# Packing the first two value parts of heads 1 to 7 into dense bf16 rows on the scalar engine, in a two-layer graph kernel

## What is computed

```
feats   = x @ W[h]                                     # 8 heads of 64 units
dense   = leaky_relu(e_self[i] + e_neigh[j], 0.2)      # e_* = feats . a_*
att     = softmax(dense where adj is 1)                # over j
x       = layernorm(x + relu(att @ feats + b))         # layer 0, heads side by side
agg     = adj @ x / max(rowsum(adj), eps)
x       = layernorm(x + relu(concat(x, agg) @ W1.T))   # layer 1
```

## Time and profile before

| what | us |
|---|---|
| median of three runs | 3327.2 |
| the profiled execution, its own time | 3327.12 |
| its span, first to last instruction | 3325.3 |
| PE busy (matmuls) | 3233.3 |
| PE weight loads busy | 2747.0 |
| vector engine busy | 2353.1 |
| scalar engine busy | 1866.8 |
| GpSimd busy | 283.5 |
| mean granted TensorE clock | 0.996 |

### The profile page before, as it was taken

One profiled execution on the slowest core, in us unless ns is written; L12 is line 12 of the kernel. 1 busy time (PEld: TensorE's weight loads), 2 busy tenths in 40 slices (PEclk: granted clock), 3 DMA queues, 4 the chain that ended last, 5 costly groups with the idle time before them and its releaser, 6 DMA issues.

```text
span 3325.3 us, 124497 instructions
## 1 busy us (share of the span) xinstructions
PE 3233.3 (97%) x56896; PEld 2747.0 (83%) x56896; DVE 2353.1 (71%) x4236; ACT 1866.8 (56%) x2456; POOL 283.5 (9%) x251
## 2 busy tenths in 40 slices
PE   4999999999999999999999999999999999999998
PEld 3978879788796978969789697897978879697895
DVE  3857858587685867858678585785858758587685
ACT  2746647365564655646466474664746647465563
POOL 0020100202002020010200102010020200202001
PEclk8999999999999999999999999999999999999999
DMA  6235251341514315252162422525135151441501
GB/s 180 73 64 149 62 138 55 92 128 57 143 61 105 108 50 151 67 111 89 50 157 67 113 88 59 150 64 131 64 79 140 57 143 50 105 119 51 135 32 51
DMA packets 368653, 314.48 MB, mean 95 GB/s; under 512 B 285056, under 2 KB 285056, under 8 KB 368128
## 3 DMA queue, kind: packets, MB, share of 16 engines
q1 hardware_dynamic: 368128, 306.52, 34.1%
HBM read 205.26 MB, written 34.08 MB: 72 GB/s over the span
## 4 chain that ended last, share of the span: by engine, by line
PE 84%; DVE 7%; DMA 5%; ACT 2%; issue 1%; SPq 0%; DVEq 0%; POOL 0%; ACTq 0%
PE six L889 73%; PE pair L889 10%; DVE mask L727 2%; DMA s_bc<-self_scores 2%; DMA out_dram<-mask 1%; DMA self_scores<-sc_row 1%; PE pair L918 1%; DVE rest L635 1%; PE six L918 1%; DVE x_parts L631 1%; ACT trh L462 1%; DVE feat L669 1%; ACT step L497 1%; DMA adj_t<-adj_word 0%; DVE trl L664 0%
## 5 line engine op out<-in xcount | busy, mean ns | idle before, releaser
L889 PE MATMUL six<-x_parts,mask 128*128 128x65 bf16 x16384 | 1547.9, 192 | 21.1 <-DVE mask L727 21.1
L889 PEld LDWEIGHTS six<-x_parts,mask 128*128 128x128 fp8e4 x16384 | 1536.8, 97 | 30.2 <-issue 20.5
L889 PE MATMUL six<-third,mask 128*128 128x65 bf16 x16384 | 1547.7, 192 | 1.9 <-issue 1.6
L889 PE MATMUL six<-rest,mask 128*128 128x65 bf16 x16384 | 1548.0, 195 | 1.3 <-issue 1.2
L889 PEld LDWEIGHTS six<-third,mask 128*128 128x128 fp8e4 x16384 | 1537.0, 98 | 2.5 <-issue 2.4
L889 PEld LDWEIGHTS six<-rest,mask 128*128 128x128 fp8e4 x16384 | 1531.7, 96 | 1.7 <-issue 0.8
L497 ACT ACTIVATE step<-s_bc,n_step 128x1024 uint16<-128x1024 f32 x1024 | 1089.1, 1137 | 378.3 <-DVE mask L727 344.7
L727 DVE TENSOR_TENSOR mask<-adj_t,step 128x1024 uint16<-128x1024 uint16 x1024 | 649.9, 685 | 60.5 <-ACT step L497 60.5
L889 PE MATMUL six<-adj_t,x_parts 128*128 128x512 fp8e4 x1536 | 385.2, 379 | 16.2 <-DVE trl L857 5.4
L440 POOL TENSOR_TENSOR s_bc<-feat,rden 128x512 f32<-128x512 f32 x112 | 124.6, 1118 | 2789.9 <-DVE s_bc L770 2776.2
L889 PEld LDWEIGHTS six<-adj_t,x_parts 128*128 128x128 f16 x1536 | 144.8, 98 | 206.1 <-issue 19.6
(11 more groups left out here) (125 smaller groups left out, 4566.9 us busy)
## 6 DMA issues: line engine op xcount, KB each, us to landing
s_bc<-self_scores SPq DMA_DIRECT2D x128, 512.0 KB, 3.8
mask<-in_adj_dram SPq DMA_DIRECT2D x64, 512.0 KB, 4.5
xs<-in_x_dram SPq DMA_DIRECT2D x128, 256.0 KB, 4.2
adj_nat<-in_adj_dram SPq DMA_DIRECT2D x64, 512.0 KB, 4.3
out_dram<-mask SPq DMA_DIRECT2D x128, 256.0 KB, 3.5
adj_nat<-in_x_dram SPq DMA_DIRECT2D x64, 256.0 KB, 5.8
step<-in_x_dram SPq DMA_DIRECT2D x64, 256.0 KB, 3.9
xs<-in_L_gnn_W_dram SPq DMA_DIRECT2D x1, 2048.0 KB, 12.3
```

The costliest lines, as they stand in the source:

```text
L889: return pe.matmul(o, l, r, start=start, stop=stop, skip_group_check=True)
```

## The change

From head 1 on (`PACKED_FROM = 1`) the scalar engine copies the first and the second part of each value into dense bf16 rows with a step of 66 numbers (132 bytes) from row to row. The tensor engine reads these in place of the upper halves. Head 0 still reads the upper halves, and the third part is as before. Each copy waits for the vector pass that makes its source (`val_f32`, `val_rest`). The two copies of head h stand on the scalar engine ahead of the step that comes five behind the mask after which the vector engine makes these values: ahead of steps 11, 17, 25, 33, 41, 49 and 57. The tensor engine waits for both before the head (`val_packed`). The first part has a buffer of its own, `packed`, and the second lies in `adj_word`, which is idle during the heads. `wa32` moves into `key_w`, which frees 256 bytes. `VALUES_AT` lists the places of the value parts, and these do not move.

```diff
@@ constants
+    PACKED_FROM = 1
...
+    VALUES_AT = {(h - 1) * T + (4 if h > 1 else 6): h for h in range(1, H)}
...
+        ROW_BF = U1 + 1
+        packed = [rows_of.rearrange("p (s k t u) -> p s k t u", s=2, k=2, t=T)[:, :, :, :, 0:U1] for rows_of in (
+            sb("packed", [P, 4 * T * ROW_BF], BF16)[:, :],
+            adj_word[:, :, :].rearrange("p s n -> p (s n)")[:, 0:4 * T * ROW_BF].bitcast(BF16))]
...
-        wa32 = sb("wa32", [P, KC, SC], F32)
+        wa32 = key_w[:, 0].rearrange("p t h -> p (t h)").rearrange("p (c n) -> p c n", c=KC)
...
+        val_packed = signal("val_packed", 2 * (H - PACKED_FROM))
@@ scalar engine
+                def pack_values(h):
+                    for part, made in enumerate((val_f32, val_rest)):
+                        act.wait_ge(made.sem, made.at(b, h + 2))
+                        copy(packed[part][:, h % 2], val[h % 2][part]).then_inc(val_packed.sem, 1)
...
                 for g in range(H * T):
+                    if g - STEP_SLOTS - 1 in VALUES_AT and VALUES_AT[g - STEP_SLOTS - 1] >= PACKED_FROM:
+                        pack_values(VALUES_AT[g - STEP_SLOTS - 1])
                     make_step(g)
@@ vector engine
-                    if jt == (4 if h else 6) and h < H - 1:
-                        value_parts(b, h + 1)
+                    if g in VALUES_AT:
+                        value_parts(b, VALUES_AT[g])
@@ tensor engine
+                    parts = val[h % 2]
+                    if h >= PACKED_FROM:
+                        parts = (packed[0][:, h % 2], packed[1][:, h % 2], parts[2])
...
-                                         val[h % 2][part][:, kind, jt, :],
+                                         parts[part][:, kind, jt, :],
...
                     pe.wait_ge(val_p2.sem, val_p2.at(b, h + 2 if h else 1))
+                    if h >= PACKED_FROM:
+                        pe.wait_ge(val_packed.sem, val_packed.at(b, 2 * (h - PACKED_FROM + 1)))
```

## The result

The changed kernel takes 3294.4 us (median of four runs, 3292.6 to 3296.2) against 3327.0 (four runs): a ratio of 0.9909, 95% interval 0.9896 to 0.9921. That is 32.5 us faster, less than half of the 67 us forecast, though inside the stated range and of the forecast sign. It lies 6 us above the rival "only the byte rate counts" (3288), and so between this rival and the free stride (3327), not between it and the forecast.

What follows compares the result with a forecast made beforehand. PE was taken as the bound, by the pitch of its 65-column matmuls in the heads. From 3327.1 us, 69 less for dense operands and 1.5 more for late masks, copies free, gave 3260 us; 8-in-10 range 3235 to 3333.

Steps and rivals of the forecast that it cites:

- only the byte rate counts: Rival for the strided matmuls of heads 1 to 7: gain only 40 us, time 3288 us; chance 0.16.
- the free stride: Rival: the 4-byte step costs nothing, something all three matmuls share sets the pitch, time 3327 us; chance 0.19.
- That PE's pitch is the time of the heads, and the moving operand's step part of it: Heads: 2064 matmuls without break, 31.21 ns each, 27.1 ns of columns; part of the rest is the operands' 4-byte step.
- The rival of a pitch that the weight load alone sets: Free-stride rival: pitch set by something shared, foremost the 98 ns weight load of each matmul; 3327 us, chance 0.19.
- The size of the stride's price: Triples of heads 1 to 7: 93.6 to 88.8 ns, 4.8 ns less, times 14336, 69 us gained.
- The 227 against 216 ns of the earlier trace: Hint from 512-column matmuls: fp32r products 227 ns against dense 216; as a rate, 1.4 ns a strided 65-column matmul.
- What is late next: Head 3, mask 29: its 0.45 us lead shrinks by 0.38 over five tiles; charged 0.1 us a batch, 1.5 in all.
- The scalar copies: Scalar engine, 224 copies of 1.15 us each, lying in idle time during the vector engine's value passes, costing nothing.
- The rival of slow copies: Rival: copies take 2.3 us each, the scalar engine becomes the bound, 3364 us; slower case in all 0.12.
- the worse reading of rows at 132 bytes: PE might read rows 132 bytes apart worse than the third part's at 144; folded into the slower case, 0.12.
- The wait of PE for masks: PE waits for a mask only at the head of a batch, 21.1 us in the run, and stays near that.
- my third hint: Inside a tile, gaps of 0.04, 0.04 behind the second part against 0.02, 0.03 behind the dense third; called weak.

## Why the prediction was wrong

**That PE's pitch is the time of the heads, and the moving operand's step part of it: right.** The rule of the Trainium skill, SBUF — State Buffer, section Door 1: The DMA port swizzle, by which a 4-byte step is free because four accesses fall in one 16-byte line, does not hold for PE's moving operand here: 1.5 ns for each 65 columns, on average over the key tiles. The rival of a pitch that the weight load alone sets falls with the same runs, since the loads stayed and the pitch fell; a share of the load in the dense 30.2 ns is not excluded.

**The size of the stride's price: the step that failed first.** I took a dense 65-column matmul at 27.1 + 2.5 = 29.6 ns, the 2.5 from 512-column streams, and gave all that was above it, 2.4 ns a matmul, to the two strided operands. Measured are 30.2 ns for a dense one and 1.5 for the step. The term was 69 us and is 44. The 227 against 216 ns of the earlier trace rows gave a nearer price (1.4 ns). I set it aside since its weights were fp32 as well, and gave the 40 us only 0.16. As no run shows that those 11 ns are the price of the stride, that it came so near may be luck. The error was to take a remainder for a price: what was above a floor carried over from matmuls eight times as long went to the one suspect I had.

**"What is late next": the second step that failed.** I charged 1.5 us, from the lead of mask 29 in the second batch and five tiles of head 3. The vector engine's chain was thought to start anew from PE's sums at each head. In heads 1 to 3 it does not: with the extra x_low passes and their 1.37 us waits it goes at a pace of its own. From mask 21, the first behind value parts, to mask 29 it is 534.54 - 521.69 = 12.85 us, and in the kernel before the same, 336.97 - 324.04 = 12.93 in the second batch and 12.85 in the third; from mask 13 to mask 21 it is 12.85 too. From tile 13 to tile 21, with two transposes on the way, PE took 8 x 1.5 + 2 x 0.47 = 12.9 us, and takes 8 x 1.45 + 0.94 = 12.5 now. From tile 21 to tile 29, with none, it took 12.0, and now has work for 11.6. In the fourth batch masks 13, 21 and 29 were there 1.06, 1.18 and 0.32 us before PE began their tiles. Now the first two are there 0.78 and 0.48 us before, and PE stands 0.83 us longer than a usual distance ahead of tile 29. Since both engines start afresh at tile 7, where PE waits for the mask, PE gains over the 21 tiles from 8 to 29, not over five: 21 x 16 x 3.1 ns = 1.04 us. At the 4.8 ns of the forecast it would have been 1.6 us a batch against a lead of 0.3, so at its own pitch the prediction should have charged some 1.3 us a batch, not 0.1. Of 7.8 us it foresaw 1.5. Two experiments bear on the cause: with the copies made and not read there is no standing at tile 29, and with the trh copies one step earlier, and nothing else changed, it is gone. It takes both the faster PE and the vector engine's wait for trh.

**The scalar copies: right in size (1.08 us against 1.15), place and cost (nothing).** The rival of slow copies falls with that; so does the worse reading of rows at 132 bytes.

**PE standing inside tiles: not in the prediction at all.** It cost 4.7 us more than before. The wait of PE for masks, which the prediction kept near 21 us, is 23.4 us in the view of waits; part of the standing at tile 29 goes there by another name.

## What to carry to other kernels

Price a change of an operand's form by the difference of two streams that differ in this form, and not by what is left above a floor; where only the remainder is at hand, test on paper what it gives when half of it belongs to something else. When the bound gets faster, follow each engine that feeds it over the whole stretch until it next waits for the bound; a lead that is there in one tile may be what is left of one that shrinks over three heads. A price per operand that is an average over places should be carried over as an average alone.

## What the runs showed that was not expected

**PE stands inside tiles, the longer in all the faster it goes.** The matmul starts of the changed kernel around one such place, in the second batch (start us, us, what):

```profile
314.56 0.20 PE L906 MATMUL six<-adj_word,mask 128*128 128x65 bf16 x1
314.60 0.19 PE L906 MATMUL six<-third,mask 128*128 128x65 bf16 x1
315.43 0.19 PE L906 MATMUL six<-packed,mask 128*128 128x65 bf16 x1 [0.65 <-issue]
```

These gaps follow transfers of the instruction queue. By the DMA records, every one of the 14 in the kernel before and of the 22 inside tiles in the changed kernel ends 2.2 to 3.1 us behind the start of such a transfer and 1.2 to 1.6 us behind its end. The transfers come some 4.0 us apart, so a band of 0.4 us is not met 36 times in 36 by chance. The one above ends 2.64 us behind the start and 1.33 behind the end.

The instruction queue's line of the page, before and after alike, says what such a transfer is:

```profile
q8 instruction: 446, 7.31, 0.9%
```

That is 16 KB each, and 113792 matmuls and weight loads over 446 are 255 instructions, 128 matmuls or some 3.9 us of the heads. The standing inside tiles grows in all the runs as the triple gets shorter: 3.7 us in all at 95.1 ns, 5.4 and 5.1 at 93.75, 5.9 and 6.8 at 92.3, 8.0 to 9.8 at 91.1, 9.9 to 10.8 at 90.6, 14.0 at 89.6.

The places are tied to the count of instructions, and not to the time. The changed kernel and the one whose copies are not read have the same PE program at different speeds, and 8 of the latter's 14 gaps come at exactly the same matmul of the same batch. The kernel before and the one with three strided operands share 9 of 14 in this way. The kernel before and the changed one, which has seven waits a batch more, share none. A place that comes again in the next batch has moved on by 15 matmuls in the kernel before and by 12 in the changed one, and seven more instructions are three and a half pairs of load and matmul. That PE has used up its instructions before the next block has arrived fits all of this, but no run changed it alone, so it is argued and not shown.

**A matmul stream has a step of its own beside the mean.** The distances inside a tile follow patterns that come back in every batch: about nine in ten of them, in most batches more, are within 2 ns of those of the third batch. With two strided operands the most frequent distances behind the first, second and third matmul of a triple are 29, 35, 29 ns, with none 32, 29, 29, and other triples of the same tile differ. A strided operand need not be slow at its own place. The gap behind the first part was as short as a dense one's (means of 30.1, 33.1 and 30.6 ns). Where the second part alone was strided the means were 30.0, 30.4 and 31.9, so most of the price stood behind the third, which is dense. So the price of one operand can be read from sums only, and my third hint, the uneven gaps of the earlier trace rows, was right that the parts matter and says nothing on the size.
